# Rotated keys: the sum of the two rotation parts by TensorE instead of a shuffle and a GpSimd sum, with new lists of steps

## The reference

```python
for i in range(4):
    x_s = attention(layernorm(x) over the 64 patches of each time)       # "s", spatial
    x_t = attention(layernorm(x + x_s) over the 16 times of each patch)   # "t", temporal
    x = layernorm(x_s + x_t) + x
t = x + first_x
out = t + experts(layernorm(t))        # 8 experts, the best 2 of each token
```

```python
x1, x2 = x[..., 0::2], x[..., 1::2]
x_rot = stack((-x2, x1), axis=-1).reshape(x.shape)
return x * cos + x_rot * sin
```

## Time and profile before

| | us |
|---|---|
| median of 3 runs | 677.92 |
| lowest, highest | 677.64, 685.77 |
| the profiled execution | 682.34 |
| its span | 680.5 |

### The profile page before, as it was taken

How to read it: one execution, slowest core, us unless ns; L and a number is a source line. 1 busy time by engine, 2 the same in 40 slices (tenths; PEclk the granted TensorE clock), 3 DMA queues, 4 the chain that set the end, 5 groups by cost and what they waited for, 6 DMA issues and landing times.

```text
span 680.5 us, 21348 instructions
## 1 busy us (share of the span) xinstructions
PE 521.3 (77%) x8936; PEld 432.0 (63%) x8936; DVE 486.6 (72%) x1400; ACT 306.9 (45%) x507; POOL 294.4 (43%) x229
## 2 busy tenths in 40 slices
PE   0788697777877877787698687787988746999992
PEld 0474676456646755575477466756776635999991
DVE  6768755978896579798856877997559875444444
ACT  1445734274567232944644346449344312333330
POOL 6514802542274043603902516148005273677552
PEclk9989769799997796999869879997798595899997
DMA  4000006600000000000001000000000013141314
GB/s 128 1 2 2 2 3 220 245 2 17 2 2 2 26 9 3 2 18 1 2 3 33 1 3 3 17 2 2 3 2 4 1 48 110 44 142 57 105 38 139
DMA packets 17281, 24.64 MB, mean 36 GB/s; under 512 B 2562, under 2 KB 12036, under 8 KB 17124
## 3 DMA queue, kind: packets, MB, share of 16 engines
q1 hardware_dynamic: 14692, 18.10, 8.3%
q0 software_dynamic: 2496, 5.18, 2.3%
HBM read 17.05 MB, written 9.33 MB: 39 GB/s over the span
## 4 chain that ended last, share of the span: by engine, by line
PE 27%; DVE 12%; issue 5%; ACT 4%; POOL 4%; DMA 1%; SPq 0%; DVEq 0%; ACTq 0%; POOLq 0%
PE score L883 6%; PE small L895 6%; PE turn L672 4%; PE score L763 3%; PE small L793 2%; POOL dispatched L534 2%; PE turn L689 2%; ACT v_t L598 1%; DVE rope L1031 1%; DVE stats L917 1%; DVE top L1046 1%; PE score L738 1%; DVE prob L1048 1%; DVE rope L1021 1%; PE small L721 1%
## 5 line engine op out<-in xcount | busy, mean ns | idle before, releaser
L486 POOL TENSOR_TENSOR rstd<-veps,mhalf 128x8 f32<-128x8 f32 x28 | 46.4, 1656 | 154.3 <-DVE veps L957 153.9
L620 ACT ACTIVATE probT<-turn 128x512 f32<-128x512 f32 x96 | 53.2, 596 | 106.6 <-PE turn L672 106.5
L1046 DVE TENSOR_REDUCE top<-score 128x16 f32<-128x1024 f32 (+1 forms) x48 | 58.5, 1219 | 46.2 <-PE score L763 46.2
L763 PE MATMUL score<-kE,qT 32*32 32x64 f32 (+1 forms) x3072 | 63.7, 286 | 21.4 <-issue 6.8
L499 POOL TENSOR_TENSOR kR<-rope,rope 128x512 f32<-128x512 f32 x32 | 41.1, 1283 | 87.7 <-issue 79.1
L763 PEld LDWEIGHTS score<-kE,qT 32*32 32x32 f32 (+1 forms) x3072 | 54.1, 136 | 35.5 <-issue 24.1
L672 PE MATMUL turn<-ident,prob 128*128 128x128 f32 x384 | 64.6, 323 | 14.3 <-ACT prob L614 14.3
L523 POOL TENSOR_TENSOR x_bias<-x_res,vec 128x1024 f32<-128x1024 f32 x16 | 37.6, 2356 | 74.6 <-DVE x_mid L1074 74.6
L672 PEld LDWEIGHTS turn<-ident,prob 128*128 128x128 f32 x384 | 52.0, 166 | 18.9 <-ACT prob L614 15.8
L1048 DVE TENSOR_TENSOR prob<-score,top 128x1024 f32<-128x1024 f32 x48 | 58.8, 1224 | 1.6
L689 PE MATMUL turn<-ident 128*128 128x128 f32 x360 | 54.7, 303 | 2.9 <-ACT xnT L583 1.9
(11 more groups left out here) (125 smaller groups left out, 1041.4 us busy)
## 6 DMA issues: line engine op xcount, KB each, us to landing
w_all<-in_w SPq DMA_DIRECT2D x2, 2048.0 KB, 20.4
dispatched<-in_slots_init SPq DMA_DIRECT2D x2, 1518.0 KB, 11.2
slots<-dispatched SPq DMA_DIRECT2D x6, 396.0 KB, 3.8
pairs<-answers SPq DMA_DIRECT2D x8, 256.0 KB, 3.8
ws<-in_w_s SPq DMA_DIRECT2D x4, 257.0 KB, 2.7
wt<-in_w_t SPq DMA_DIRECT2D x4, 257.0 KB, 2.5
x_in<-in_x SPq DMA_DIRECT2D x2, 512.0 KB, 4.2
vec<-in_vec_in SPq DMA_DIRECT2D x4, 256.0 KB, 4.4
```

Source lines behind the costliest of these rows:

```text
L486: nc.gpsimd.tensor_tensor(rstd[:, q.nth % 4, :], veps[:, q.nth % 4, :], mhalf[:, :], ALU.pow).then_inc(rstd_ready, 1)
L620: nc.scalar.activation(probT[:, q.nth % 2, 2 * k:2 * k + 2, 2 * h:2 * h + 2, :].rearrange("p k g n -> p k (g n)"), turn[:, u % 2, :].rearr ...
L763: last = nc.tensor.matmul(score[b * n:(b + 1) * n, g, c * 2 * n:(c + 1) * 2 * n], qT[rows, tok:tok + n], kE[rows, :, tok:tok + n], start=q ...
L1046: nc.vector.tensor_reduce(tops, mine, AX_X, ALU.max).then_inc(top_ready, 1)
```

## The change

The sum for the keys is made by TensorE. VectorE now multiplies the key's bank by the cosine table (into rope1) and by the sine table (into rope2), both straight from the bank, with no shuffle. A new step, *fold*, multiplies rope1 by the identity and rope2 by a matrix exch, minus the identity with each pair of columns swapped, and adds both up in one turn bank. ScalarE's masked copies (part) read that bank. GpSimd's sum for the keys, its tile kR and the semaphore key_ready are gone; the queries are treated as before, except for the counts in the waits. Exch is one more load of 64 KB at the start. The bank of a key tile is now free after two products of VectorE (rope_done). All lists are new, among them the number of fillers: 8 instead of 9 in ORDERS, 11 instead of 18 in TAIL.

```diff
     "PE": """
-        score.s00 head.t10- mix.t10- score.s01 head.s00 out.t10- mix.s00 head.s01 mix.s01 glow.s03 out.s00
-        turn.s10 glow.s02 project.s10 turn.t00 project.t00 glow.s11 values.s10 values.t00 score.s10 head.s10
-        score.s11 mix.s10 head.s11 score.t00 mix.s11 out.s10 glow.s01 head.t00 glow.s05 glow.s07 mix.t00
-        turn.t10 project.t10 out.t00 score.t10 glow.s09 values.t10 glow.s04 turn.s00+ project.s00+ values.s00+
-        glow.s10
+        score.s00 glow.s06 head.t10- mix.t10- head.s00 score.s01 out.t10- mix.s00 head.s01 mix.s01 glow.s05
+        out.s00 turn.s10 project.s10 turn.t00 fold.s10 values.t00 project.t00 values.s10 score.s10 fold.t00
+        score.s11 head.s10 mix.s10 score.t00 head.s11 mix.s11 glow.s02 out.s10 glow.s07 glow.s01 glow.s03
+        head.t00 mix.t00 turn.t10 project.t10 out.t00 fold.t10 score.t10 values.t10 glow.s04 turn.s00+ glow.s00
+        project.s00+ fold.s00+ values.s00+
     "ACT": """
-        out.s00 normal.s10 turn.s10 normal.t00 turn.t00 part.s10 values.s10 values.t00 soft.s10 part.t00
-        head.s10 rest.s10 mix.s10 soft.s11 head.s11 rest.s11 mix.s11 soft.t00 out.s10 head.t00 rest.t00 mix.t00
+        out.s00 normal.s10 turn.s10 normal.t00 turn.t00 values.t00 part.s10 values.s10 soft.s10 part.t00
+        rest.s10 head.s10 mix.s10 soft.s11 rest.s11 head.s11 soft.t00 mix.s11 out.s10 rest.t00 head.t00 mix.t00
     "POOL": """
-        bias.s00 stats.f10- stats.s10 stats.t00 project.s10 project.t00 bias.f00 bias.s10 bias.f10 stats.t10
-        project.t10 stats.f00 stats.s00+ project.s00+
+        bias.s00 stats.f10- stats.s10 stats.t00 project.s10 project.t00 bias.s10 bias.f00 stats.t10 project.t10
+        stats.f00 stats.s00+ project.s00+ bias.f10
...
@@ GpSimd, project
-                        pool.wait_ge(rope_done, tile + 1)
-                        if tile >= 2:
-                            pool.wait_ge(key_ready, tile - 1)
-                        nc.gpsimd.tensor_tensor(kR[:, tile % 2, :], rope1[:, (2 * tile) % 4, :],
-                                                rope2[:, (2 * tile) % 4, :], ALU.add).then_inc(rope_sum, 1)
-                        pool.wait_ge(swapped, 2 * tile + 2)
+                        pool.wait_ge(swapped, tile + 1)
@@ ScalarE, part
-                        act.wait_ge(rope_sum, 2 * tile + 1)
+                        act.wait_ge(turn_full, u + 1)
                         for e in range(2):
-                            last = nc.scalar.activation(kE[:, e, cols], kR[:, tile % 2, :], ACT.Copy, scale=hmask[:, e:e + 1])
-                        last.then_inc(key_ready, 1)
+                            last = nc.scalar.activation(kE[:, e, cols], turn[:, u % 2, :], ACT.Copy, scale=hmask[:, e:e + 1])
+                        last.then_inc(turn_free[u % 2], 1)
@@ TensorE
+                elif q.step == "fold":
+                    proj = STEPS["project", q.layer, q.kind, q.half, 0].proj
+                    for t in range(2):
+                        tile, u = proj // 2 + t, q.turns + t
+                        if u >= 2:
+                            wait_read(pe, turn_free, u - 2)
+                        pe.wait_ge(rope_done, 2 * tile + 1)
+                        nc.tensor.matmul(turn[:, u % 2, :], ident[:, :], rope1[:, 2 * tile % 4, :], start=True, stop=False)
+                        pe.wait_ge(rope_done, 2 * tile + 2)
+                        nc.tensor.matmul(turn[:, u % 2, :], exch[:, :], rope2[:, 2 * tile % 4, :], start=False,
+                                         stop=True).then_inc(turn_full, 1)
@@ VectorE, project
-                    for j in range(4):
-                        i = q.proj + j
-                        if i >= 4:
-                            dve.wait_ge(rope_sum, i - 3)
-                        dve.wait_ge(proj_full, i + 1)
-                        nc.vector.stream_shuffle(rope2[:, i % 4, :], score[:, i % 4, :], SWAP).then_inc(swapped, 1)
-                        nc.vector.tensor_tensor(
-                            rope1[:, i % 4, :].rearrange("p (s n) -> p s n", n=length),
-                            score[:, i % 4, :].rearrange("p (s n) -> p s n", n=length),
-                            table[:, 0, None, :].broadcast_to([P, BANK // length, length]), ALU.mult).then_inc(proj_free, 1)
-                        if j % 2 == 0:
-                            by_sine(i)
+                    for t in range(2):
+                        tile = q.proj // 2 + t
+                        if tile >= 2:
+                            dve.wait_ge(turn_full, FOLD[tile - 2] + 1)
+                        dve.wait_ge(proj_full, 2 * tile + 1)
+                        times(rope1, 2 * tile, 0).then_inc(rope_done, 1)
+                        times(rope2, 2 * tile, 1).then_inc(rope_done, 1)
+                        if tile >= 2:
+                            dve.wait_ge(rope_sum, tile - 1)
+                        i = 2 * tile + 1
+                        dve.wait_ge(proj_full, i + 1)
+                        nc.vector.stream_shuffle(rope2[:, i % 4, :], score[:, i % 4, :], SWAP).then_inc(swapped, 1)
+                        times(rope1, i, 0).then_inc(proj_free, 1)
+        "exch": -np.eye(P, dtype=np.float32)[np.arange(P) ^ 1],
```

More of the change, by code:

```diff
@@ L90 @@
 TAKES = {
-    "PE": ("glow", "turn", "values", "project", "score", "head", "mix", "out", "logits", "place", "tick"),
+    "PE": ("glow", "turn", "values", "project", "fold", "score", "head", "mix", "out", "logits", "place", "tick"),
     "DVE": ("stats", "normal", "final", "project", "soft", "rest", "divide", "out", "rank", "place", "origin", "tick", "merge"),
@@ L146 @@
[L146 removed]
+        divide.t10@0 divide.t11@0 out.t10@0 stats.f10@0 final.f10@0 stats.e10@0 rank.e10@0 normal.e10@0
+        origin.e00@0 place.e10@0 origin.e10@21 merge.e00@47 merge.e10@47
     """,
     "ACT": """
[L149 to L151 removed]
+        head.t10-@0 soft.s00@0 mix.t10-@0 rest.s00@0 out.t10-@0 head.s00@0 mix.s00@0 soft.s01@0 rest.s01@0
@@ L152 @@
+        head.s01@0 mix.s01@0 out.s00@0 normal.s10@0 turn.s10@0 normal.t00@0 turn.t00@0 part.s10@0 values.t00@0
+        values.s10@0 part.t00@0 soft.s10@0 rest.s10@0 head.s10@0 mix.s10@0 soft.s11@0 rest.s11@0 head.s11@0
         soft.t00@0 mix.s11@0 rest.t00@0 out.s10@0 head.t00@0 mix.t00@0 normal.t10@0 turn.t10@0 out.t00@0
-        part.t10@0 values.t10@0 turn.e00@0 soft.t10@0 rank.e00@0 rest.t10@0 normal.e00@0 head.t10@0 mix.t10@0
-        out.t10@0 turn.e10@0 normal.e10@0 rank.e10@0
+        part.t10@0 values.t10@0 turn.e00@0 soft.t10@0 rank.e00@0 head.t10@0 rest.t10@0 normal.e00@0 mix.t10@0
@@ L276, in metaformer @@
         rope2 = at("rope2", [P, 4, BANK], 8192)
[L277 removed]
+        exch = at("exch", [P, P], 19968)
         qT = at("qT", [P, TOKENS], 20480)
```

86 lines of the change are left out of this document (46 added, 40 removed).

## The result

The changed kernel takes 675.11 us (median of 12 runs, 671.84 to 677.05), the kernel before on the same chip 681.21 (12 runs): a ratio of 0.990, 95% interval 0.988 to 0.993. That is faster, by 1 per cent, where 3.4 per cent were forecast. By the prediction's own measure, where a difference under 2 per cent counts as the same, it is "same", to which it gave 0.24; its range for 8 in 10 (640 to 676 us) holds the time only because it was drawn wide enough to take in rival 3. The profiled executions are 673.99 and 682.34, their spans 672.1 and 680.5.

The account below looks back on a forecast made before the run. Waits at handovers bound the kernel, neither VectorE nor TensorE being full, with TensorE at half clock in two stretches per layer. Terms summed to -28.2 us, +4.8 for pauses left -23.4: 654.5 against 677.9; 8-in-10 range 640 to 676.

Parts of the forecast that it names:

- rival 3: The handovers keep their times, Stretch A gives 0 and stretch B half: 675.5 us; chance 0.13.
- stretch B: From the wait for the last rotated queries to the next layer's scores: full clock and earlier transposes, -10.0 us.
- TensorE's scores waiting for the masked keys: Named sign of being wrong: TensorE's scores wait for ScalarE's masked key copies; no size given.
- Stretch A: Around the first scores of the patches' second half: earlier scores, hole filled by fold.t00, clock kept up; -20.8 us.
- the walk: Step-by-step timing of Stretch A with layer 2's times: 25.3 us from score.s10 to out.s10's products, against 29.93.
- The allowance of +4.8: One new pause of 1.2 us per layer, because 16 more steps are handed over: +4.8 us.
- Rival 2: TensorE's clock falls all the same, folds run at half clock: +24.8 us, 703 us; chance 0.10.
- Bias: GpSimd's bias.f10 no longer stands in front of the variance step, in three layers: -2.0 us.
- Head.s00 ahead of score.s01: In TensorE's list, delays scores VectorE waits on by 0.9 us in three layers: +2.7 us.
- the row for C: From project.s00 to project.s10, three layers: the forecast terms assigned there come to +1.2 us.
- The start: Nothing covers the fold there; score.s00 stands behind fold.s00 and the values, with VectorE done: +3.1 us.
- The end: From project.t10 of layer 3 on: a gain from that layer's last step of rotation, -1.2 us.

Follow-up runs that it names:

- values_first: The changed kernel with values.t10 moved ahead of score.t10 in TensorE's list, in three layers: 670.27 us, ratio 0.979 to the kernel before.
- after_mid: The changed kernel with four identity products between the two halves of each t score: 676.0 us, ratio 0.988 to the kernel before.
- new_fill_b: The changed kernel with two fillers between fold.t10 and score.t10 in three layers: 677.1 us, ratio 0.993 to the kernel before.
- old_fill_a: The kernel before with four more fillers behind score.s10 in all four layers: 678.83 us, ratio 0.991.
- fold_half: The changed kernel with each fold doing only the identity times the cosine part, sine part left out: 675.0 us, ratio 0.988 to the kernel before.
- values_mid: The values_first kernel with four identity products between the halves of each t score: 668.7 us, ratio 0.979 to the kernel before.

## Why the prediction was wrong, point by point

**The step that failed** is stretch B's "scores from 390.0 instead of 389.31, but at full clock: to 394.3; values.t10 and one filler (two before) to 397.5". The start was right in kind (12.3 us after project.t10, forecast 12.0), VectorE was on time, and the clock wasn't: from score.t10 to the transposes 12.1 us on average, forecast some 8.5, before 12.0. I had walked over an idle of 1.3 us for the masked keys and put the pauses and the clock behind it at nothing, as if only the holes that I was closing could bring the clock down. In layer 1 this is 2.2 us of pauses and 3.6 of half clock. The fold moved the fall of the clock behind the start of the scores, and in layer 1 with it its return, from the values to behind the filler. TensorE's scores waiting for the masked keys was one of the signs of being wrong that the prediction named, and it came. Nothing came of the 10.6 us of this row; values_first, by order alone, brings the distance to 8.4 to 9.6 us, with the values already done, and B down by some 6. What brings the clock down in the scores stays open: the wait for the keys and the pauses are each missing in some case, the row of small products is there in all, but no run changes it alone.

**Stretch A** has the mechanism right and one term mis-sized. Up to score.s10 -5.2 for -4.8. From there to out.s10's products -9.5 for -16.0: score.s11 comes as walked (6.2 us behind score.s10, walked 6.1), but from score.t00 on the clock is down for 3.4 us and more, which the walk had kept at full: after_mid, with a full clock there, has 25.7 and 25.5 in layers 0 and 1 where the walk has 25.3. I had carried the pause of the earlier trace rows along with its length and without the clock behind it. Layer 3 is another matter, 28.5 in after_mid too: its own list has values.s10 between score.s10 and fold.t00, so score.s11 comes 8.1 us behind score.s10, and I had taken the walk of the other layers for it.

**The allowance of +4.8** for new pauses is 8.2 by what TensorE sat idle (6.8 us in front of the scores' products before, now 10.5 and three times 1.51 for the keys), and it had no price for what follows each.

**Rival 2**, the fall of the clock, had the mechanism of the failure and the wrong place: not at the folds, all sixteen of which run at full clock (their pairs of records take 1.02 to 1.13 us), but behind them. The Trainium skill (TensorE: Matmul & The Clock Gate, "HAM oscillation") has the clock go down at each of the waits for data that come round between groups of products. The traces agree in part: the holes of 3.2 and 4.0 us before are such waits, but in new_fill_b the clock falls with no idle ahead of it. **Rival 3** gave the time, 675.5, by luck, with a story that is wrong: the handovers did move, A gave 16.6 of it, and B lost 3.4.

**The other terms.** Bias -2.0, as forecast: the variance step takes 0.17 in all layers, 0.84 in three before. Head.s00 ahead of score.s01, +2.7: the row for C is right by its sum, but undoing the order gave nothing, so the term was wrong; what does make C longer is not settled. New half-clock stretches there (0.57 from 300 to 304 us) are a candidate, no run isolates them. The start: score.s00 begins 2.2 us later (31.16), not 3.1, and project.s10 1.4. The end: +1.8 for -1.2; score.t10 of layer 3 has two pauses, 1.10 and 1.55, and half clock behind them, as in B.

**Where the expected gain went**, then: of A's 16.6 us, 9.5 lie where the hole was filled (old_fill_a has as much without the change, and fold_half, with the hole back, has none of it: 119.0 for 119.1), 2.0 are the bias step's, and 5.2 the shorter rotation's in its new order (with the old order project.s10 to score.s10 takes 19.0 in layers 0 to 2, not 17.6); B's saving on VectorE, some 1 us a layer, stands behind a TensorE that comes 1.9 to 4.0 us late.

## What to carry to other kernels

Work that fills a hole is paid for by the clock, and work that doesn't costs nearly all of its time: halving the folds gained 2 of 27 us here, doubling them cost 52 of 55. When a gap is closed, follow the granted clock to the next wait, the next pause and the next dense row of small products before counting on it, and put work that waits for nothing (the values) between an engine's wait and its dense stretch of small products. A change of arithmetic has to be judged with its lists: with the old ones this one was 5 per cent slower, with one more swap of two words it is 1.7 to 2.1 per cent faster, the best version that was run (values_first at 670 us; values_mid at 669 can't be told from it).

## What the runs showed of the hardware

The pauses named "issue" in TensorE's dense stretches (0.4 to 2.3 us) sit on a grid in the instruction stream. In the changed kernel 54 steps of 125.2 records lie between 1094 and 7857, and the instruction queue of the page has 73 packets for 8,984 products, one for 123, and 16.4 KB each (1.20 MB):

```profile
q8 instruction: 73, 1.20, 0.7%
```

The Trainium skill (Runtime: NRT & Kernel Launch, "Instruction fetch mechanics") tells of blocks of 16 KiB, 256 instructions, that the engine fetches while it runs the one before, and calls the crossing mostly hidden. A product and its weight load are two instructions, so by an estimate from that figure a block is 128 products, or a few less with other instructions between them: the distance and the size of a packet agree. "Hidden" doesn't where products are small: 75 to 128 of them take 1.0 to 1.5 us in the t scores, and there the crossing shows. That the pause is the wait for that fetch is argued from the distance and the packets, not shown; that it is tied to the stream is shown. No run found a rule for its length, and at many places of the grid no pause shows.

The granted clock falls in the t scores also where no idle time stands ahead of the fall (new_fill_b layer 0, the kernel before layer 2), and stays at 1.00 in score.t00 where four larger products stand in the middle (all 12 cases; in score.t10 it falls with them too). And a wait for another engine can stand under "issue": the 1.51 us before score.t10 end with the key copies, 0.20 us behind them.
